# Start-up of a two-layer recurrent and attention kernel: the angles' sine moved from ScalarE to GpSimd, the weight splits put in order of use

## The reference

```python
nu = softplus(nu_log); mag = exp(-exp(nu)); theta = exp(theta_log)      # 32 states
A_re, A_im = mag * cos(theta), mag * sin(theta)
gamma = sqrt(clip(1 - mag * mag, 0))
Bu_re, Bu_im = x @ (gamma * B_re).T, x @ (gamma * B_im).T
h_t = A * h_(t-1) + Bu_t                                                # complex, over 256 steps
y = H_re @ C_re.T - H_im @ C_im.T + D * x
...
h = gelu(x @ proj1.T + proj1_bias)                                      # 256 -> 1024, exact gelu
out = h @ proj2.T + proj2_bias
```

## Time and profile before

| what | us |
|---|---|
| median of 3 runs | 803.28 |
| lowest, highest | 803.16, 805.17 |
| the profiled execution | 803.25 |
| its span | 801.4 |
| TensorE busy | 781.8 |
| VectorE busy | 699.8 |
| ScalarE busy | 523.6 |
| GpSimd busy | 466.3 |

### The profile page before, as it was taken

How to read it: one execution, slowest core, us unless ns; L and a number is a source line. 1 busy time by engine, 2 the same in 40 slices (tenths; PEclk the granted TensorE clock), 3 DMA queues, 4 the chain that set the end, 5 groups by cost and what they waited for, 6 DMA issues and landing times.

```text
span 801.4 us, 23023 instructions
## 1 busy us (share of the span) xinstructions
PE 781.8 (98%) x7912; PEld 716.3 (89%) x7912; DVE 699.8 (87%) x2647; ACT 523.6 (65%) x1612; POOL 466.3 (58%) x1245
## 2 busy tenths in 40 slices
PE   7999999999999999999999999999999999999978
PEld 5988999888889889899998999899999998999957
DVE  6898787887788899999898999999999899998885
ACT  4554455455563787777767777677777777777672
POOL 6833022022334686775868668686776867769653
PEclk9999999999999999999999999999999999999999
DMA  8610011000001322232222322223222222322210
GB/s 304 243 32 4 1 67 67 1 1 1 2 10 35 55 45 44 53 58 46 51 39 47 57 52 51 38 45 58 51 54 37 46 48 54 59 38 47 44 40 29
DMA packets 101333, 41.15 MB, mean 51 GB/s; under 512 B 91744, under 2 KB 98400, under 8 KB 100576
## 3 DMA queue, kind: packets, MB, share of 16 engines
q1 hardware_dynamic: 98896, 38.89, 21.8%
q10 hardware_dynamic: 2320, 0.79, 0.4%
HBM read 14.47 MB, written 4.19 MB: 23 GB/s over the span
## 4 chain that ended last, share of the span: by engine, by line
PE 82%; DVE 6%; POOL 5%; SPq 3%; issue 2%; ACT 1%; DMA 1%; ACTq 0%; POOLq 0%; DVEq 0%
PE bank L522 57%; PE bank L728 10%; PE bank L750 8%; PE bank L721 2%; POOL SM L1972 2%; PE bank L586 1%; SPq L416 1%; SPq L487 1%; POOL par L1811 1%; PE bank L596 1%; DVE PT L1593 1%; PE bank L636 1%; DVE SM L1570 1%; PE bank L539 1%; POOL QA L1965 1%
## 5 line engine op out<-in xcount | busy, mean ns | idle before, releaser
L1019 ACT ACTIVATE SM<-SM,stb 128x32 f32<-128x32 f32 (+7 forms) x512 | 206.1, 404 | 65.9 <-DVE stb L1570 61.4
L1972 POOL TENSOR_SCALAR SM<-SM,stb 128x32 f32<-128x32 f32 (+7 forms) x512 | 195.0, 400 | 78.8 <-DVE stb L1577 77.3
L522 PE MATMUL bank<-yh,wq_lo 128*128 128x256 f32 x512 | 150.5, 294 | 0.0
L522 PE MATMUL bank<-yh,wq_hi 128*128 128x256 f32 x512 | 144.7, 283 | 0.0
L522 PE MATMUL bank<-yl,wq_hi 128*128 128x256 f32 x512 | 144.5, 282 | 0.0
L728 PE MATMUL bank<-KT,QT 128*128 128x192 f32 (+4 forms) x640 | 121.1, 328 | 3.1 <-DVE stb L1570 3.1
L1570 DVE CUSTOM_DVE_ANT_0 SM<-bank,CONST 128x224 f32<-128x224 f32 (+3 forms) x320 | 97.0, 346 | 22.1 <-PE bank L728 19.5
L728 PEld LDWEIGHTS bank<-KT,QT 128*128 128x128 f32 x640 | 97.5, 190 | 6.8 <-DVE stb L1570 5.1
L1593 DVE STREAM_TRANSPOSE PT<-SM 128x128 f32<-128x128 f32 (+2 forms) x232 | 99.5, 460 | 3.0 <-PE bank L750 2.7
L522 PEld LDWEIGHTS bank<-yh,wq_lo 128*128 128x128 f32 x512 | 97.1, 190 | 1.4
L522 PEld LDWEIGHTS bank<-yh,wq_hi 128*128 128x128 f32 x512 | 97.0, 190 | 0.0
(11 more groups left out here) (218 smaller groups left out, 2080.7 us busy)
## 6 DMA issues: line engine op xcount, KB each, us to landing
QT<-QA SPq DMA_DIRECT2D x240, 64.0 KB, 2.1
PT<-KV SPq DMA_DIRECT2D x256, 16.0 KB, 1.8
out<-fo SPq DMA_DIRECT2D x32, 128.0 KB, 2.0
X<-in_x SPq DMA_DIRECT2D x7, 512.0 KB, 10.7
stage<-in_wqn SPq DMA_DIRECT2D x2, 1024.0 KB, 9.8
stage<-in_wo SPq DMA_DIRECT2D x2, 1024.0 KB, 5.0
stage<-in_w1t SPq DMA_DIRECT2D x4, 256.0 KB, 5.4
stage<-in_w2t SPq DMA_DIRECT2D x2, 512.0 KB, 6.3
```

Of the source, the lines that this page charges most:

```text
L522: i = e.matmul(dst, a, b, start=(first and j == 0), stop=(last and j == 2), skip_group_check=skip)
L1019: i = e.activation(M[:, at], M[:, at], ACT.Exp, bias=S[:, 0, j:j + 1], scale=-1.0, accum_out=S[:, 1, j:j + 1])
L1972: i = e.tensor_scalar(P[:, at], P[:, at], S[:, 2, j:j + 1], 1.0, ALU.mult, ALU.mult)
```

## The change

1. **Sine.** ScalarE's `angles` and its semaphores go. GpSimd evaluates sine and cosine of the half angles by polynomials in a new tile `trig` (seven coefficients each, set by 14 memsets at the start), in 15 operations where nine followed the sine before. The empty activation ahead of ScalarE's loop is now a gelu.
2. **Splits.** The parts of w1 are split in steps 0, 2, 4 (before all in step 0), those of w2 in 1, 3, 5, 6 (before 1, 2, 3, 5 on ScalarE and 1, 2, 3, 6 on VectorE), b in 5 and 6 (before 3 and 4). The norm of chunk 1 starts in step 2.
3. **First block.** `l0_first` is `l0_up(0, 0)` with the products that need the low part of x last.
4. **Scan.** The first scan moves from step 9 to 10, its `l0_bu` from 5 to 7, its y from 10 and 11 to 12 and 13; for chunk 1 bu and scan move from 12 to 14, y from 14 to 16 and 16 to 17; the first transposes of chunks 1 and 2 one step later; `l0_out` of chunk 0 from 14 to 15.
5. **Magnitude.** Four pieces a step from step 5, after the x splits, in place of seven from step 4.
6. **Tables.** `RR` is scaled after tci and tsi; the scan waits for two tables, y for the third. The rope constants move to step 9, behind the roots of chunk 2 (l0_roots in step 8; the third chunk by count).

```diff
+TURN_FIRST = (5, 13, 20, 28, 36, 44, 52)
+BU_AT = (7, 14, 20, 28, 36, 44, 52, 60)
+SCAN_AT = (10, 14, 20, 28, 36, 44, 52, 60)
+Y_AT = ((12, 16, 22, 30, 38, 46, 54, 62), (13, 17, 23, 31, 39, 47, 55, 63))
 L0_STEPS = 70
 RING = 6
 
...
+            def l0_first():
+
+
+                sl = slice(0, 128)
+                w.wait_ge("w1h", 1)
+                w.wait_ge("w1l", 1)
+                for k in range(2):
+                    w.wait_ge("xth", k + 1)
+                    e.matmul(fbank[0][:, :], w1l[:, k, sl], xh[0][:, k, :], start=(k == 0), stop=False)
+                    e.matmul(fbank[0][:, :], w1h[:, k, sl], xh[0][:, k, :], start=False, stop=False)
+                for k in range(2):
+                    w.wait_ge("xtl", k + 1)
+                    i = e.matmul(fbank[0][:, :], w1h[:, k, sl], xl[0][:, k, :], start=False, stop=(k == 1))
+                i.then_inc(SEM["f1"], 1)
+
...
             def l0_y(c, b):
+                w.wait_ge("tab", 3)
...
-                if g < 8 * NC:
+                if g == 0:
+                    l0_first()
+                elif g < 8 * NC:
                     l0_up(g // 8, g % 8)
-                if g in (5, 12, 20, 28, 36, 44, 52, 60):
-                    c = (5, 12, 20, 28, 36, 44, 52, 60).index(g)
-                    l0_bu(c)
-                if g in (10, 14, 22, 30, 38, 46, 54, 62):
-                    c = (10, 14, 22, 30, 38, 46, 54, 62).index(g)
-                    l0_y(c, 0)
+                if g in BU_AT:
+                    l0_bu(BU_AT.index(g))
+                if g in Y_AT[0]:
+                    l0_y(Y_AT[0].index(g), 0)
...
                     l0_turn(c + 1, 1)
-                c, r = divmod(g - 4, 8)
-                if r == 0 and 0 <= c < NC - 1:
+                if g in TURN_FIRST:
+                    c = TURN_FIRST.index(g)
                     l0_turn(c + 1, 0)
...
 
-            def angles():
-                w.wait_ge("ang", 1)
-                w.wait_ge("sin", 1)
-                e.activation(col(48, 16), col(32, 16), ACT.Sin).then_inc(SEM["sin"], 1)
-
             def m_high():
                 w.wait_ge("wm", 80)
                 e.activation(LB[0][:, :], lbs, ACT.Copy).then_inc(SEM["lbh"], 1)
...
             w.wait_ge("par", 1)
-            e.activation(col(56), tsn[:, 0:1], ACT.Sin).then_inc(SEM["sin"], 1)
+            e.activation(trig[:, 15, 0:1], tsn[:, 0:1], ACT.Gelu)
             w1_high(0)
             x_high(0, 0)
             x_high(0, 1)
...
                     gate_exp(0)
-                if g == 3:
+                if g == 5:
                     b_high()
-                if g == 0:
-                    w1_high(1)
-                if g == 0:
-                    w1_high(2)
-                if g == 0:
-                    w1_high(3)
+                if g in (0, 2, 4):
+                    w1_high(1 + g // 2)
                 if g == 65:
                     mids(0, wbank)
                 if g == 55:
                     y_high(0, wbank)
-                if g == 0:
-                    angles()
-                if g == 1:
-                    w2_high(0)
-                if g == 2:
-                    w2_high(1)
-                if g == 3:
-                    w2_high(2)
-                if g == 5:
-                    w2_high(3)
+                if g in (1, 3, 5, 6):
+                    w2_high((1, 3, 5, 6).index(g))
                 if g == 38:
                     o_high(0, 0)
                 if g == 46:
...
                 if g == 30:
                     nope_high(1, 1)
 
-                c, r = divmod(g - 4, 8)
-                if r == 0 and 0 <= c < NC - 1:
+                if g in TURN_FIRST:
+                    c = TURN_FIRST.index(g)
                     x_high(c + 1, 0)
                 c, r = divmod(g - 6, 8)
                 if r == 0 and 0 <= c < NC - 1:
...
                 w.wait_ge("bu", c + 1)
-                w.wait_ge("tab", 3)
+                w.wait_ge("tab", 2)
                 w.wait_ge("mag", 1)
                 w.wait_ge("zz", 2 * c)
                 w.wait_ge("rot", count["rot"])
...
                     l1_norm(1)
-                if g == 1:
-                    w2_low(0)
-                if g == 2:
-                    w2_low(1)
-                if g == 3:
-                    w2_low(2)
-                if g == 6:
-                    w2_low(3)
+                if g in (1, 3, 5, 6):
+                    w2_low((1, 3, 5, 6).index(g))
                 if g == 58:
                     l1_kv(0)
                 if g in (7, 13, 21, 29, 37, 45, 53, 61):
...
                     skip(c, 1)
-                if g == 0:
-                    w1_low(1)
-                if g == 0:
-                    w1_low(2)
-                if g == 0:
-                    w1_low(3)
-                if g in (9, 12, 20, 28, 36, 44, 52, 60):
-                    c = (9, 12, 20, 28, 36, 44, 52, 60).index(g)
+                if g in (0, 2, 4):
+                    w1_low(1 + g // 2)
+                if g in SCAN_AT:
                     go(make)
-                    scan(c)
+                    scan(SCAN_AT.index(g))
                 if g == 65:
                     mids_low(0, wbank)
-                if g in (10, 14, 22, 30, 38, 46, 54, 62):
-                    c = (10, 14, 22, 30, 38, 46, 54, 62).index(g)
-                    states_out(c, 0)
-                if g in (11, 16, 23, 31, 39, 47, 55, 63):
-                    c = (11, 16, 23, 31, 39, 47, 55, 63).index(g)
-                    states_out(c, 1)
+                if g in Y_AT[0]:
+                    states_out(Y_AT[0].index(g), 0)
+                if g in Y_AT[1]:
+                    states_out(Y_AT[1].index(g), 1)
                 c, r = divmod(g - 9, 8)
...
                     norm = l0_norm(1)
-                go(norm, 4)
+                go(norm, {2: 1, 3: 4}.get(g, 9))
                 if g == 65:
                     turn_queries(0, 0)
                 if g == 66:
                     turn_queries(0, 1)
-                if g == 4:
+                if g == 6:
                     b_low()
                 if g == 58:
                     gate = l1_gate(0)
                 go(gate, 4)
-                if g == 4:
-                    make = magnitude()
-                go(make, 7)
                 if g < 8 * NC:
                     h_low(g)
-                c, r = divmod(g - 4, 8)
-                if r == 0 and 0 <= c < NC - 1:
+                if g in TURN_FIRST:
+                    c = TURN_FIRST.index(g)
                     x_low(c + 1, 0)
                 c, r = divmod(g - 6, 8)
                 if r == 0 and 0 <= c < NC - 1:
                     x_low(c + 1, 1)
+                if g == 5:
+                    make = magnitude()
+                go(make, 4)
                 if g == 26:
                     m_low()
                 if g == 54:
...
                     nope_low(1, 1)
-                if g in (14, 24, 29, 37, 45, 53, 61, 69):
-                    c = (14, 24, 29, 37, 45, 53, 61, 69).index(g)
+                if g in (15, 24, 29, 37, 45, 53, 61, 69):
+                    c = (15, 24, 29, 37, 45, 53, 61, 69).index(g)
                     l0_out(c, 0)
-                if g in (14, 24, 29, 37, 45, 53, 61, 69):
-                    c = (14, 24, 29, 37, 45, 53, 61, 69).index(g)
+                if g in (15, 24, 29, 37, 45, 53, 61, 69):
+                    c = (15, 24, 29, 37, 45, 53, 61, 69).index(g)
                     l0_out(c, 1)
                 if g == 38:
                     o_low(0, 0)
...
 
+            ODD, EVEN, SUMS, PAIRS = (trig[:, i:i + n, :] for i, n in ((0, 3), (3, 3), (6, 4), (10, 2)))
+            q1, q2, q4 = (trig[:, i, :] for i in (12, 13, 14))
+            for k in range(7):
+                at = SUMS[:, 3, :] if k == 6 else (ODD if k % 2 else EVEN)[:, k // 2, :]
+                e.memset(at[:, 0:8], float((-1) ** k / math.factorial(2 * k + 1)))
+                i = e.memset(at[:, 8:16], float((-1) ** k / math.factorial(2 * k)))
+            i.then_inc(SEM["par"], 1)
+            done[0] += 1
+
             w.wait_ge("nuth", 16)
             exact_exp(col(1), col(3), None)
             turns(col(24), col(3))
...
             ts(r8, r8, PI, -PI, ALU.min, ALU.max)
-            w.wait_ge("par", done[0])
-            e.tensor_scalar(ab, r8, 0.5, None, ALU.mult, ALU.bypass).then_inc(SEM["ang"], 1)
             exact_exp(col(0), col(2), "nu")
 
 
-            s8, c8, w8, v8 = col(48, 8), col(56, 8), col(32, 8), col(40, 8)
-            w.wait_ge("sin", 2)
-            tt(c8, c8, c8, ALU.mult)
-            ts(c8, c8, -2.0, 1.0, ALU.mult, ALU.add)
-            tt(w8, s8, s8, ALU.mult, free=True)
-            tt(v8, c8, c8, ALU.mult)
-            tt(w8, w8, v8, ALU.add)
-            ts(w8, w8, -0.5, 1.5, ALU.mult, ALU.add)
-            tt(s8, s8, w8, ALU.mult)
-            tt(c8, c8, w8, ALU.mult, free=True)
-            ts(v8, s8, -1.0, 1.0, ALU.mult, ALU.mult)
+            s8, c8, v8 = col(48, 8), col(56, 8), col(40, 8)
```

(38 more changed lines are left out.)

13 lines of the change are left out of this document (7 added, 6 removed).

## The result

| | kernel before | changed kernel |
|---|---|---|
| median | 803.26 (22 runs) | 804.94 (22 runs) |
| lowest, highest | 802.72, 806.43 | 803.12, 807.33 |
| the profiled execution | 803.25 | 807.33 |
| its span | 801.4 | 805.5 |

A forecast was written before the change was run, and what follows sets the result against it. TensorE, busy 98% of the span, bounds the kernel, but VectorE's backlog decides: of 6.6 us removable 1.95 is left, other parts cost 0, so 803.25 becomes 801.3 us, called "same"; range 798.3 to 803.7.

The forecast's parts named there:

- what comes free at the start: TensorE's 3.1 us wait for ScalarE's gelu, plus 1.5 us of lower clock and 0.3 us in the first block.
- that VectorE then decides: From about 14 us VectorE's backlog, not TensorE's account, sets the time, leaving 1.95 of 6.6 us.
- the layout: VectorE's new order timed from old trace rows, up to step 18 at 71.85 us; error 0.45 us.
- Both just fit: cost 0: GpSimd's tables ready at 42.1 (wanted 42.6), chunk 2's roots at 48.2 (wanted 48.55): cost 0, bound 0 to 4.8 us.
- tables a little late: Rival: slower sine operations start the scan 1 to 2 us late, 802.0 to 803.3, or a reloaded table, 802.6; together 0.18.
- the slower rival: Rival: GpSimd's polynomial becomes the bound at 0.85 us per operation, scan 4.8 us late, 806.1 us; chance 0.06.
- a wait of 1.5 us costs 1.5 us: TensorE's new waits for VectorE, 0.65 to 1.55 us, priced at their length, without any fall of the clock.
- the waits behind 75 us: TensorE's later waits, none over 2.6 us at once, lie where nothing is edited, so they count nothing.
- nobody waits for them: GpSimd's rope constants, moved behind chunk 2's roots, are not needed before step 59; the move was given no gain.
- The two accounts: TensorE's account of at most 6.6 us to remove, and VectorE's account leaving 1.95 us.
- the five waits: TensorE waiting for VectorE between 24 and 71 us: 1.1, 1.05, 1.55, 1.0 and 0.65 us.
- the chain: VectorE's operations laid end to end up to step 18's up block: 71.85 for 73.80, so 1.95 us gained.

The follow-up runs named there:

- e1: Changed kernel with 8 of the 15 operations of GpSimd's sine polynomial left out (wrong rotation): median 802.63 us, ratio 0.9988 to the kernel before.
- e10: Changed kernel with GpSimd's exponential for nu and its sine issued in turn, same output: median 804.87 us, ratio 1.0004 to the kernel before.
- e6: Kernel before with 20 unused matmuls filling TensorE's gap before the last block: median 803.62 us, ratio 1.0001 to the kernel before.
- e5: Changed kernel with 20 unused matmuls filling TensorE's gap before the last block: median 804.52 us, ratio 1.0015 to the kernel before.
- e12: Changed kernel with GpSimd's rope constants put back ahead of chunk 2's roots: median 805.81 us, ratio 1.003 to the kernel before.

## Why the prediction was wrong

**Right: what comes free at the start.** ScalarE's sine and its table load gone, gelu 0 at 12.60 (12.6 forecast), low half 0 at 14.05 (14.07), clock 1.00 from 15 to 20. **Right: that VectorE then decides.** Low half 9 ended within 0.2 us of the layout, and once GpSimd is out of the way (e1) the scan starts within 0.04 and step 18 within 0.36, an error that I had put at 0.45 for the layout. VectorE's waits for y and bu, 0.9 and 0.8 forecast, are 0.79 and 0.86 in e1.

**Wrong, first step: "Both just fit: cost 0".** The polynomial itself was sized well (15 operations in 6.95 us, 7.5 forecast), and so were the doublings (13.0, 13.1 forecast). What failed stood around them. tsi ended at 43.45 for 42.1: 0.1 us of the 1.35 had gathered by the end of the doublings, 0.3 passed between them and tci, and 0.96 came from the two tables, which took 0.98 each and not 0.5. The scan started at 43.53 for 42.6; chunk 2's roots took 6.3 us for 5.4 and ended at 50.25 for 48.2. The sum of 0.93 and 0.68 at VectorE is 1.6 us, and e1, which takes both away, gives 73.89 − 72.21 = 1.7 at step 18. The rival "tables a little late" had the consequence, at 0.18, with 802.0 to 803.3; it looked for the cause in the sine, and it left out that the roots behind the tables are late too.

The tables took 0.47 and 0.55 in the kernel before, and there VectorE wasn't pausing. It ran the statistics of a chunk, which read one operand in SBUF:

```profile
39.23 1.39 DVE L1227 BATCH_NORM_STATS2 st<-X 128x6 f32<-128x256 f32 x4
...
39.64 0.47 POOL L1895 TENSOR_SCALAR tci<-CS,par 128x256 f32<-128x256 f32 x1
40.10 0.55 POOL L1896 TENSOR_SCALAR tsi<-CS,par,CONST 128x256 f32<-128x256 f32 x1
```

In the changed kernel they fall beside low half 9 and the skip, two 512-wide tensor_tensors with two SBUF inputs, the second of which took 0.88 for the usual 0.69. Other runs agree. tci took 0.48 us in e1, while VectorE stood still until 40.16, and 0.48 in e10, beside the sums (`z<-bank,VEC`, one input in PSUM); tsi took 1.06 in e10 beside low half 9. The Trainium skill (SBUF — State Buffer, the section Who interferes with whom) states that such an instruction and a GpSimd instruction that reads SBUF contend; the rows agree. The tables' cost is read from rows, though; no run moves them alone.

The same happened to the exponential for nu. In the kernel before its first four operations were

```profile
15.31 1.17 POOL L1811 TENSOR_SCALAR par<-par 128x1 f32<-128x1 f32 x4
```

beside statistics and small operations of VectorE. In the changed kernel they started 1.1 us earlier, at 14.24, behind the clamp at 13.96, and ended at 16.57, beside low half 0, a w2 split and low half 1. The whole exponential took 7.1 us for 5.5, so the sine started at 21.27 and not at 20.45, although GpSimd had been early. I had counted one operation less in front of the sine, and no change of the time of the others. What I had weighed for the polynomial alone in the slower rival, that GpSimd's operations grow where VectorE runs 512-wide tensor_tensors, was right, and it struck the operations before and behind it.

**Wrong, second step: a wait of 1.5 us costs 1.5 us.** I had priced the clock's fall at the old place (1.5 us) and given it back in full, but priced the new waits at their length. Even the old price isn't paid in every run (e6: step 18 at 73.14 with the fall elsewhere), so up to 0.7 us of the 1.95 forecast hung on which execution I had as a profile. The two waits at steps 12 and 13, 1.1 and 2.07 us with 5.5 us between them, bring the clock down in a part of the runs, and then cost 1.6 us more (e5 against the changed kernel). GpSimd's lateness made the second one 2.07 instead of 1.55 (1.27 without it, in e1). In the profile of e1, the clock held, and in that of e12, with 2.9, it fell; that a longer wait brings the fall more often is likely by these, not shown.

**Wrong, third step: the waits behind 75 us "move along with everything else and are no part of the sum".** The gap before the last block moves along, but what the clock does behind it differs from run to run by 0 to some 3 us: filling it takes the two kernels' spreads from 4.2 and 3.7 to 2.0 and 1.9. It has about the same place in the kernel before, so a part of its runs pay it too.

**The account.** Forecast of the profiled execution: step 18 at 71.85. GpSimd's lateness 1.7, the layout's error 0.36: 73.9, nothing gained on the kernel before's 73.80, which fits the fastest runs, 803.12 and 802.72. The fall at 55 us: 1.6, gives 75.5 (75.48 measured). For the median the sum is: forecast 801.3; fastest run 803.12, 1.8 more, which is the first step and the layout; median 804.94, another 1.8, which is the clock at the two places. In the kernel before, median and fastest run are only 0.5 apart. 75.48 − 73.80 = 1.7 of the 4.1 us of difference in span stand before step 18; the other 2.4 are behind it, 2.2 of them behind the start of the last block's first small matmuls (764.73 to the end of the span 40.8 us, 762.84 and 38.6 in the kernel before).

**Also wrong by its price.** The rope constants' place on GpSimd was put at nothing ("nobody waits for them"); by e12 it is a microsecond or more, since what it clears is the way of chunk 2's roots, which are wanted at once. **Two smaller faults of the working.** The two accounts don't agree: 6.6 less the five waits (5.35) leaves 1.25, the chain leaves 1.95, and e1's profile has 1.6 (73.80 to 72.21). And the remaining splits of w1 ran on VectorE from 11.90 to 14.26 in the kernel before, while TensorE was busy, not inside its pause from 14.5.

**The slower rival** (the polynomial as the bound, 806.1) did not happen in the polynomial: an operation took 0.46 us, under its point of 0.5 to 0.63. The median between 803.7 and 806.1 came from three smaller costs, of which I had only one as a rival.

## What to carry to other kernels

When a change moves one engine's work in time, the durations of its neighbours from the old trace no longer hold. Size an operation of GpSimd by rows of the old trace that have the same kind of VectorE instruction beside it (here: two inputs in SBUF, or not), and do so for the operations before and behind the edited ones too. Where two chains "just fit", give the miss its full consequence, with everything queued behind it, instead of zero. And a wait of TensorE has two prices, its length and, if it brings the clock down, here another 1.5 or 1.6 us, paid in some runs and not in others, in the kernel before as well. Compare kernels by their fastest runs and by the mean granted clock as well as by the median, and look for gaps far behind the edit that can go either way.

## What the runs showed of the hardware that I had not expected

- The same two waits of 1.1 and 2.07 us at the same times led to a granted clock of 0.66 from 55 to 60 us in one execution and of 1.00 in another. The Trainium skill (TensorE: Matmul & The Clock Gate, Part 1: The HAM clock gate) calls the number of slow matmuls at a kernel's start variable from run to run; here the same holds in mid-kernel.
- One gap of 2.3 us near 767 us, some 37 us before the end, is behind differences of up to some 3 us between executions of one kernel.
- The width of a GpSimd operation says little about its time in this stretch. In the changed kernel between 21 and 28.3 us, by shape (count, busy, mean ns):

```profile
L1809 POOL TENSOR_TENSOR trig<-trig 128x16 f32<-128x16 f32 x4 | 2.7, 669 | 0.2
L1809 POOL TENSOR_TENSOR trig<-trig 128x48 f32<-128x48 f32 x2 | 0.9, 465 | 0.2
...
L1803 POOL TENSOR_SCALAR par<-par 128x8 f32<-128x8 f32 x3 | 0.6, 216 | 0.1
```

The mean of the 16-wide ones is that of one: it stood from 24.91 to 26.95, while VectorE ran low half, w2 split and low half one behind the other (24.98, 25.58, 26.18); the other three took some 0.2 us each. An 8-wide tensor_scalar took 0.22 us here and 0.85 in the earlier trace rows.

- The longest such case stands in the same profile, where it costs nothing. A tensor_scalar of 32 columns that took 0.21 us at 40.77 in the kernel before took

```profile
51.39 3.85 POOL L1909 TENSOR_SCALAR rope_s<-CONST 128x32 f32<-128x32 f32 x1
```

while VectorE went through the rope constants' split, a gate and low half 11 without a pause, all with two inputs in SBUF. It ended at 55.24, with the last of them (55.15). So one GpSimd operation can stand behind several VectorE instructions in a row, and not only behind one.
